# Replanning the recurrence: one feed-forward piece behind nearly every scan step, one dense run of 16 at group 1

## The reference, cut to what matters

```python
# x: (4, 1024, 128) float32
x = x + 0.5 * ffn(layernorm(x))          # attention + mixture of experts
x = x + hierarchical_attention(layernorm(x))
x = x + 0.5 * ffn(layernorm(x))
x = x + 0.5 * binary_ffn(layernorm(x))   # "a": h = gelu(x W1 + b1); h W2 + b2, 128 -> 512 -> 128
y = layernorm(x)                         # "p"
# scan over time, 1024 steps, state of 32 numbers for each of 4 sequences
state_t = tanh(state_{t-1} @ A.T + y_t @ B.T)
mixed_t = state_t @ C.T + y_t @ D.T
r = layernorm(mixed + y) * w + b         # "r"
x = x + r + gelu(r W1 + b1) W2 + b2
x = x + 0.5 * binary_ffn(layernorm(x))   # "z"
```

## Time and profile before

| | us |
|---|---|
| median of 3 runs | 2276.3 (2274.05 to 2276.82) |
| span of the profiled execution | 2273.6 |
| start of the scan (first tanh) | 1341.25 |
| the eight groups of the scan, first to last tanh | 885.4 |
| drain, from the last tanh to the end | 46.9 |
| PE busy, of the span | 1783.6 (78%) |
| ACT busy, of the span | 861.1 (38%) |

### The profile page before, as it was taken

One profiled execution on the slowest core, in us unless ns is written; L12 is line 12 of the kernel. 1 busy time (PEld: TensorE's weight loads), 2 busy tenths in 40 slices (PEclk: granted clock), 3 DMA queues, 4 the chain that ended last, 5 costly groups with the idle time before them and its releaser, 6 DMA issues. The chain is left out here.

```text
span 2273.6 us, 39093 instructions
## 1 busy us (share of the span) xinstructions
PE 1783.6 (78%) x13672; PEld 1353.0 (60%) x13672; DVE 1010.2 (44%) x3005; ACT 861.1 (38%) x2377; POOL 193.0 (8%) x314
## 2 busy tenths in 40 slices
PE   2889895838778497849989956979788887879775
PEld 1666674537575474726666644757666665757554
DVE  3666654866776777647666521111112121211101
ACT  1444443646556465424434322223222323232222
POOL 1212201000010010021112000000000000000000
PEclk8999996979889698869999955555555555555556
DMA  6000000000000000000000000000000000000000
GB/s 153 1 1 1 0 1 1 2 1 3 2 2 3 1 2 2 2 1 1 1 1 0 1 1 1 1 5 1 5 2 6 1 5 1 5 1 5 1 5 5
DMA packets 12029, 13.20 MB, mean 6 GB/s; under 512 B 1648, under 2 KB 10640, under 8 KB 11280
## 3 DMA queue, kind: packets, MB, share of 16 engines
q1 hardware_dynamic: 11840, 10.77, 1.8%
HBM read 8.67 MB, written 2.10 MB: 5 GB/s over the span
## 5 line engine op out<-in xcount | busy, mean ns | idle before, releaser
L965 ACT ACTIVATE r_state<-r_scan 32x4 f32<-32x4 f32 x1024 | 166.1, 162 | 647.8 <-PE r_scan L907 647.8
L907 PE MATMUL r_scan<-r_state,rnnA 128*32 128x4 f32 x2048 | 274.6, 204 | 157.8 <-ACT r_state L965 150.2
L907 PEld LDWEIGHTS r_scan<-r_state,rnnA 128*32 128x32 f32 x2048 | 187.5, 140 | 310.5 <-ACT r_state L965 219.1
L286 PEld LDWEIGHTS f_down<-moe,f_hT 128*128 128x128 f32 x2048 | 251.8, 195 | 57.1 <-issue 53.9
L277 PE MATMUL f_up<-f_x2T,moe 128*128 128x512 f32 x512 | 248.3, 609 | 11.6 <-ACT f_hT L193 11.6
L286 PE MATMUL f_down<-moe,f_hT 128*128 128x128 f32 x2048 | 254.7, 278 | 0.0
L463 DVE SCALAR_TENSOR_TENSOR x_all<-f_down,f_weight,x_all 128x128 f32 (+1 forms) x512 | 144.0, 344 | 166.7 <-PE f_down L286 164.0
L193 ACT ACTIVATE f_hT<-f_up 128x512 f32<-128x512 f32 x256 | 149.9, 598 | 138.9 <-PE f_up L277 137.5
L1579 DVE TENSOR_TENSOR att_big<-at_ring,att_big 128x512 f16<-128x512 f32 x192 | 123.9, 685 | 48.9 <-ACT att_big L1261 48.1
L277 PEld LDWEIGHTS f_up<-f_x2T,moe 128*128 128x128 f32 x512 | 90.3, 194 | 89.9 <-issue 63.5
L1261 ACT ACTIVATE att_big<-at_ring 128x512 f16<-128x512 f32 x192 | 111.4, 596 | 66.2 <-PE at_ring L1394 64.3
(11 more groups left out here) (241 smaller groups left out, 3171.9 us busy)
## 6 DMA issues: line engine op xcount, KB each, us to landing
x_all<-in_x SPq DMA_DIRECT2D x4, 512.0 KB, 6.2
moe<-in_moe SPq DMA_DIRECT2D x2, 1024.0 KB, 6.3
out<-x_all SPq DMA_DIRECT2D x8, 256.0 KB, 2.3
bin<-in_bin SPq DMA_DIRECT2D x2, 256.0 KB, 7.5
mlp<-in_mlp SPq DMA_DIRECT2D x2, 256.0 KB, 6.1
att_big<-in_att_wq SPq DMA_DIRECT2D x1, 512.0 KB, 10.7
att_big<-in_att_wk SPq DMA_DIRECT2D x1, 512.0 KB, 12.7
att_big<-in_att_wv SPq DMA_DIRECT2D x1, 512.0 KB, 14.6
```

The lines of the kernel that those rows point to most:

```text
L286: last = nc.tensor.matmul(down[e % 2][:, s * 128:(s + 1) * 128], hT[c % H_RING][:, s * 128:(s + 1) * 128], w2[:, c * 128:(c + 1) * 128], s ...
L907: nc.tensor.matmul(scan[b][0:STATE, NB * t:NB * (t + 1)], rnnA[:, :], last, start=False, stop=(t == 127), skip_group_check=True).then_inc( ...
L965: nc.scalar.activation(state[b][0:STATE, NB * t:NB * (t + 1)], scan[b][0:STATE, NB * t:NB * (t + 1)], ACT.Tanh).then_inc(s_tanh, 1)
```

## The change

The plan is one table for all groups, with one piece to a step, spread over steps 0 to 125. Work for a moves one group earlier: body g now carries a of group g+2 (before g+1), and the prologue does a of groups 0 and 1. A function `early` changes the steps in the groups of `BURST`, which is group 1 alone: the 16 pieces of steps 0 to 15 all go behind step 0, and every later piece 11 steps earlier. The gelus get a table of their own, one to a step. The loops of all engines are gone: eight groups are written out, with constant semaphore values and constant group indices. DVE's and POOL's orders follow the new plan. Count and shape of all computing instructions stay.

```diff
-            UP_A = [6, 7, 8, 9, 18, 19, 22, 23]
...
-                p += [((60 if i < 4 else 62) + i // 2, down_piece, (pe, "z", g, i)) for i in range(16)]
...
+            SLOTS = {
+                "turn_a": [0, 1, 2, 3], "mix": list(range(4, 12)),
+                "up_a": list(range(12, 22)) + [50, 51, 52, 53, 54, 55],
+                "turn_p": [22, 23, 24, 25], "turn_r": [26, 27, 28, 29], "input": [30, 31, 32, 33],
+                "up_r": list(range(34, 50)), "down_r": list(range(56, 72)),
+                "down_a": list(range(72, 84)) + [88, 89, 106, 107], "turn_z": [84, 85, 86, 87],
+                "up_z": list(range(90, 106)), "down_z": list(range(110, 126)),
+            }
+            BURST, AT_ONCE = (1,), 16
+
+            def early(g, slot):
+
+                return slot if g not in BURST else 0 if slot < AT_ONCE else slot - AT_ONCE + 5
+
+            GELU_A, GELU_R, GELU_Z = [16, 20, 54, 58], [38, 42, 46, 50], [94, 98, 102, 106]
...
-                body(0, 0, False, True)
-                with pe.Fori(0, GROUPS // 2 - 1) as i:
-                    body(2 * i + 1, 1, True, True)
-                    body(2 * i + 2, 0, True, True)
-                body(GROUPS - 1, 1, True, False)
...
+                pieces(turn_piece, NB, "a", 0)
+                pieces(up_piece, 16, "a", 0)
+                pe.wait_ge(s_nT["a"], ONE + 1)
+                pieces(turn_piece, NB, "a", 1)
+                pe.wait_ge(s_nT["a"], ONE + 2)
+                pieces(down_piece, 16, "a", 0)
+                pieces(up_piece, 16, "a", 1)
+                pieces(turn_piece, NB, "p", 0)
+                pieces(input_piece, NB, 0)
+                pieces(down_piece, 16, "a", 1)
+                pe.wait_ge(s_zero, ONE + 1)
+                for g in range(GROUPS):
+                    body(g)
```

More of the change, by code:

```diff
@@ L674, in rsqrt @@
                 def rsqrt(k, g):
+                    if not 0 <= g < GROUPS:
+                        return
                     pool.wait_ge(s_stats[k], ONE + g + 1)
@@ L681, in rsqrt, with v_stats @@
                                        ALU.pow).then_inc(s_root[k], 1)
[L683 to L697, removed]
+                rsqrt("a", 0)
+                rsqrt("a", 1)
+                rsqrt("p", 0)
+                rsqrt("a", 2)
+                rsqrt("p", 1)
+                for g in range(GROUPS + 1):
+                    rsqrt("r", g - 1)
+                    rsqrt("a", g + 3)
+                    rsqrt("z", g - 1)
+                    rsqrt("p", g + 2)
             @block.vector
             def _(dve):
-                def v_stats(k, src):
+                def v_stats(k, g, src):
                     for s in range(NB):
@@ L812, in up_piece @@
                     if k == "a" and c < 2:
-                        if last_z is not None:
-                            pe.wait_ge(s_h["z"], ONE + FC * last_z)
+                        pe.wait_ge(s_h["z"], ONE + FC * max(g - 3, 0))
+                        pe.wait_ge(s_h["a"], ONE + FC * g - (2 - c if g else 0))
                     elif k == "r" and c < 2:
@@ L898, in run, with body @@
                             f(*args)
[L900 to L902 removed]
+                def body(g):
+                    b = g % 2
+                    plan = plan_of(pe, g)
                     for t in range(128):
@@ L909, in body, with pieces @@
                         run(plan, t)
-                pre = plan_pre(pe, 0, 0, None)
-                for t in range(128):
-                    run(pre, t)
-                pe.wait_ge(s_zero, ONE + 1)
-                body(0, 0, False, True)
-                with pe.Fori(0, GROUPS // 2 - 1) as i:
-                    body(2 * i + 1, 1, True, True)
-                    body(2 * i + 2, 0, True, True)
-                body(GROUPS - 1, 1, True, False)
-                post = plan_post(pe, GROUPS - 1, 1, GROUPS)
-                for t in range(128):
-                    run(post, t)
+                def pieces(f, n, *args):
+                    for i in range(n):
+                        f(pe, *args, i)
+                pieces(turn_piece, NB, "a", 0)
[10 more added lines that the diff above has]
+                for g in range(GROUPS):
+                    body(g)
+                plan = plan_of(pe, GROUPS)
+                for t in range(128):
+                    run(plan, t)
             @block.scalar
@@ L956, in run, with body @@
                             gelu_piece(*args)
-                def body(g, b, post, pre):
-                    plan = plan_gelus(g - 1 if post else None, g + 1 if pre else None)
-                    if post:
+                def body(g):
+                    b = g % 2
+                    plan = plan_gelus(g)
+                    if g >= 2:
                         act.wait_ge(s_out, ONE + g - 1)
@@ L967, in body @@
                         run(plan, t)
-                plan = plan_gelus(None, 0)
-                for t in range(128):
-                    run(plan, t)
-                body(0, 0, False, True)
-                with act.Fori(0, GROUPS // 2 - 1) as i:
-                    body(2 * i + 1, 1, True, True)
-                    body(2 * i + 2, 0, True, True)
-                body(GROUPS - 1, 1, True, False)
-                plan = plan_gelus(GROUPS - 1, None)
+                for g in range(2):
+                    for c in range(FC):
+                        for s in range(NB):
+                            gelu_piece("a", g, c, s)
+                for g in range(GROUPS):
+                    body(g)
+                plan = plan_gelus(GROUPS)
                 for t in range(128):
```

161 lines of the change are left out of this document (92 added, 69 removed).

## The result

The changed kernel takes 2225.65 us (2222.99 to 2229.54) against 2276.56 for the kernel before: ratio 0.978, interval 0.9765 to 0.9793, faster. The forecast was 2230. Its profiled execution has a span of 2224.9 us and took 2226.66.

What follows compares the result with a forecast made beforehand. Bound: at 0.5 clock, the chain scan product to tanh to scan product, stretched by TensorE's pieces between. Span 2273.6 - 52.0 (groups) + 5.3 (prologue) = 2226.9 us; the median stands 2.7 above, so 2230, range 2195 to 2255.

Steps and rivals of the forecast that it cites:

- Step prices: Scan steps with one piece at the low clock: FFN 0.92 us, transpose 0.60, mix 0.97, input 0.53, bare 0.52.
- Small waits: Waits inside each full group, taken over from the kernel before: 1.1 us a group.
- Groups: The eight groups of the scan, priced one by one: sum 833.4 us against 885.4, so -52.0.
- Group 0: First group of the scan: 80.0 us against 84.0, with a's transposes no longer waiting for DVE at step 0.
- Prologue: Ahead of the scan, 36 more pieces: up pieces cost 0 in idle time, down pieces 5.3 us.
- The term 5.3: The prologue's 16 down pieces ahead of the first scan product: 5.3 us, between 3.6 (high clock) and 7.0 (low).
- Drain: The drain, with the same pieces and the same chain: 46.9 us.
- The clock: TensorE's clock in the scan: no rise expected from group 1's dense run of transposes, mix and FFN pieces.
- Rival B: Single FFN steps are dearer: slower than before if above 0.99 us, 2294 us in all at 1.02; chance 0.07.
- Rival C: Chains of gelus and norms too tight: 3 us more in each of seven groups, 2251 us; chance 0.10.
- Rival A: Dense run raises the clock, one piece a step holds it: 2040 us, or 2205 for one group; chance 0.13.
- Spreading: FFN pieces one to a step: nearly neutral at the low clock, 1.84 us a pair against 1.87.

Runs made afterwards that it cites:

- e1: The changed kernel without the dense run in group 1; 2220.13 us, ratio 0.976.
- e2: The changed kernel with its dense run replaced by r's 16 down pieces behind step 56 in groups 1 to 7; 2193.05 us, ratio 0.964.
- e7: e6 with the added matmuls on 32 rows instead of 128; 2358.1 us, ratio 1.035.
- e5: The dense runs of e2 and the added matmuls of e6 together; 2095.8 us, ratio 0.920.
- e9: e5 with two added matmuls behind each mix piece instead of one; 2052.6 us, ratio 0.901.
- e12: e9 with the mix pieces spread over steps 4 to 16, FFN pieces between them; 2065.8 us, ratio 0.907.
- e6: e1 with one more 128-row matmul, its product unused, behind each bare step, transpose or mix piece; 2211.4 us, ratio 0.972.
- e4: e1 with its pieces paired again, two behind one step and the next bare; 2254.77 us, ratio 0.990.
- e8: e6 with the added 128-row matmul behind bare steps alone; 2195.5 us, ratio 0.964.
- e10: e6 with two added matmuls behind each mix piece, no dense run; 2222.3 us, ratio 0.977.
- e3: The kernel before with its loops written out on all four engines, nothing else changed; 2266.62 us, ratio 0.996.

## Why the prediction was right

- *Step prices* held: FFN 0.92 by subtraction, 0.93 measured; transpose 0.60, measured 0.61; mix 0.97, measured 0.96 to 0.97; input 0.53 and bare 0.52, as measured. Taking one dense piece off the pair gives the step with one piece.
- *Small waits* were over-sized: 1.1 us a group was taken over from before. With the measured prices a full group is 16 x 0.61 + 8 x 0.965 + 96 x 0.927 + 4 x 0.53 + 4 x 0.52 = 110.7, against 110.64: nothing is left. The predicted 111.0 is so near because two errors cancel in part: the rounded-down prices were 0.8 us low in the sum, the waits 1.1 us too high. The one wait foreseen, z's down pieces at step 110, shows as a step of 0.98 instead of 0.93, 0.05 us and not 0.3.
- *Groups*: 114.0 predicted for group 1, 113.7 measured; 444.0 for groups 2 to 5, 442.6; 97.9 and 97.5 for groups 6 and 7, 97.3 and 96.4. The sum was 833.4, measured 831.1.
- *Group 0* was under-sized, 80.0 against 81.1. The prediction had the wait at its step 0 gone. It is still there, now for DVE's update of a:

```profile
1345.94 0.23 PE L941 MATMUL r_scan<-r_state,rnnA 128*32 128x4 f32 x2
1347.65 0.30 PE L860 MATMUL r_pre_misc<-ident,r_xn_a 128*128 128x128 f32 x1 [1.49 <-DVE x_all L735]
1347.88 0.23 PE L941 MATMUL r_scan<-r_state,rnnA 128*32 128x4 f32 x2
```

  The transpose waits 1.49 us and the next scan product waits behind it, so the step takes 1.94 us instead of 0.60. Part is given back by the short high clock there (transpose steps of 0.48).
- *Prologue*: the start of the scan, 1346.20 against 1346.5, was met partly by luck. The term 5.3 was taken between a price at the high and one at the low clock, and no execution shows that value. In the profiled execution the clock fell at 1337.7, ahead of them, and rose only at 1344.5; in that of e1, with the same prologue, it stayed high:

```profile
1340.05 5.96 PE L845 MATMUL r_pre_misc<-bin,r_h_pre 128*128 128x128 f32 x32
1339.26 3.84 PE L845 MATMUL r_pre_misc<-bin,r_h_pre 128*128 128x128 f32 x32
```

  (the changed kernel, then e1). Of the twelve profiled executions five took near 5.96 us for them, six 3.84 and one 4.36. From the prologue's first transpose to the first tanh it is 29.0 us in the five, 25.8 in the six, against 23.2 before: the prologue costs 5.9 or 2.6 us. That is 3.2 of the 7 us by which the start varied; the rest lies ahead of that first transpose (1316.5 to 1321.1), and no run explains it.
- *Drain* 47.6 against 46.9. The span was 2224.9 against 2226.9. The other 2 us lie in the step from span to median: +2.7 was taken from before, and here it is 0.75.
- *The clock*: no rise from the dense run, as argued from the 64-row matmuls and the mix pieces. e2 is the proof from the other side: 16 FFN pieces in a row raise it. The reading of the rows (64-row and mix matmuls don't count for as much) is borne out by the dense run; how far it is the number of rows stays open, as said at e7.
- *Rival B* is out: an FFN step is 0.93 and not 0.99. *Rival C* is out: but for step 0 of group 0, TensorE waits in the groups for nothing but the tanh, at most 0.3 us at a time. *Rival A* fell on its first half only. Its second half, that one FFN piece to a step holds the clock, came true in part: in e2 and e5 such steps run at the high clock, at 0.57 us (0.65 estimated), with a bare step at 0.48 (0.46 estimated), but e9 and e12 lose the clock in rows of them. In the changed kernel nothing raises it inside the scan; had it risen, e2 and e6 suggest that transposes or mix pieces would have lost it.

Spreading was called nearly neutral for FFN pieces, and is: of e4's 115.1 us less e1's 110.7, the FFN pairs make 48 x (1.35 + 0.52 - 1.86) = 0.5. Transposes, mix and input make 8 x 0.13 + 4 x 0.32 + 2 x 0.42 = 3.2 (the prediction's "three quarters" were 3.2 of its 4.6), and the rest is small waits.

Open: why e9 and e12 lose the clock at different steps of groups with the same instructions, whether rows or columns per us decided e7, and whether transposes count less than other matmuls. In e2 the fall comes among four of them, but they are also the sparsest steps there, so the runs do not separate the two.

## What to carry to other kernels

Price a step that doesn't exist yet by taking one piece off the pair that the trace shows, and leave out waits that belonged to the old order. A dense run only pays if its content raises the clock and what follows keeps it: look at what stands behind the run before adding one. In a chain with idle TensorE time between its steps, 128-row matmuls put into the gaps were worth more here, together with a dense run, than the reordering (173 us on top of 51); without the dense run they brought 9 (e6).

## What the runs showed of the hardware

- A 128-row float32 matmul with 32 columns of weights, behind a bare scan product, is hidden at the low clock (step 0.52 us either way, e8); with 32 rows it makes the step 0.76 (e7).
- At the low clock some five such steps of 0.52 us raised it (e8, 1396.8), where single FFN steps of 0.93 us, as busy, never did.
- Busy time doesn't tell whether the clock will be granted: 99.00 us of 99.00 busy in e7 at 0.50, 56.16 of 62.40 in e6 at 1.00.
- A full group costs 110.6 us at the low clock without added work, 123.0 with it (e10), 80.6 at the high clock with it (e9). Added work that fails to hold the clock loses 12 us a group, work that holds it gains 30.
- The jump back of this hardware loop cost TensorE 3.3 us, twice in a launch (e3).
